# Causal scores masked after the exponential by GpSimd for two of four groups of heads, with small steps of the second attention layer moved

## What is computed

```python
q = q * cos + _rotate_half(q) * sin            # 16 heads of depth 8, 256 tokens
k = k * cos + _rotate_half(k) * sin
att = jnp.einsum('bhtd,bhsd->bhts', q, k) * scale
causal = jnp.tril(jnp.ones((T, T), dtype=bool))
att = jnp.where(causal, att, jnp.finfo(att.dtype).min)
att = jax.nn.softmax(att, axis=-1)
y = jnp.einsum('bhts,bhsd->bhtd', att, v)
y = y.transpose(0, 2, 1, 3).reshape(B, T, C)
return y @ w_proj
```

## Time and profile before

| | us |
|---|---|
| time before, median of 3 runs | 1256.86 (1255.71 to 1260.93) |
| the profiled execution's own time | 1255.29 |
| its span, first instruction to last | 1253.5 |
| PE busy | 1060.1 (85%) |
| DVE busy | 924.8 (74%) |
| ACT busy | 848.4 (68%) |
| POOL busy | 625.6 (50%) |

### The profile page before, as it was taken

How to read it: one execution, slowest core, us unless ns; L and a number is a source line. 1 busy time by engine, 2 the same in 40 slices (tenths; PEclk the granted TensorE clock), 3 DMA queues, 4 the chain that set the end, 5 groups by cost and what they waited for, 6 DMA issues and landing times. The chain is left out here.

```text
span 1253.5 us, 35551 instructions
## 1 busy us (share of the span) xinstructions
PE 1060.1 (85%) x11349; PEld 784.8 (63%) x11349; DVE 924.8 (74%) x2432; ACT 848.4 (68%) x1920; POOL 625.6 (50%) x894
## 2 busy tenths in 40 slices
PE   4699999999999999687899999999999996921420
PEld 3467666666667676365687877888778884511420
DVE  3488888888888888153577777777777773479895
ACT  2267777777777777473577887778877775632596
POOL 3245556655556553306355666556665531500494
PEclk9699999999999999798799999999999998865655
DMA  7555545555545552027656556555555540300013
GB/s 197 125 141 130 137 122 128 132 132 131 128 122 133 132 130 53 2 106 239 165 151 153 147 146 150 148 152 147 147 148 146 146 95 15 115 9 0 1 43 92
DMA packets 120217, 148.39 MB, mean 118 GB/s; under 512 B 12467, under 2 KB 99923, under 8 KB 110931
## 3 DMA queue, kind: packets, MB, share of 16 engines
q1 hardware_dynamic: 113362, 139.65, 44.0%
q10 hardware_dynamic: 6784, 7.86, 1.9%
HBM read 88.44 MB, written 45.35 MB: 107 GB/s over the span
## 5 line engine op out<-in xcount | busy, mean ns | idle before, releaser
L528 DVE TENSOR_REDUCE attn_negmax<-attn_row_ps 128x2 f32<-128x512 f32 (+1 forms) x1024 | 597.0, 618 | 189.0 <-PE attn_row_ps L718 177.8
L450 ACT ACTIVATE probs<-attn_col_ps 128x512 f32<-128x512 f32 (+1 forms) x1024 | 530.6, 541 | 129.9 <-PE attn_col_ps L740 122.1
L718 PE MATMUL attn_row_ps<-k_st,q_st 72*128 72x256 bf16 (+1 forms) x2048 | 369.5, 262 | 8.0 <-DMA k_st<-attn_scratch 8.0
L740 PE MATMUL attn_col_ps<-q_st,k_st 74*128 74x256 bf16 (+1 forms) x2048 | 367.4, 260 | 2.7 <-ACT probs L450 1.5
L757 PE MATMUL attn_out_ps<-probs,v_sb 128*32 128x256 f32 (+1 forms) x4096 | 228.5, 356 | 0.7 <-ACT probs L450 0.7
L740 PEld LDWEIGHTS attn_col_ps<-q_st,k_st 74*128 74x128 bf16 x2048 | 186.8, 98 | 63.7 <-ACT probs L450 30.3
L718 PEld LDWEIGHTS attn_row_ps<-k_st,q_st 72*128 72x128 bf16 x2048 | 201.1, 99 | 34.3 <-issue 8.6
L757 PEld LDWEIGHTS attn_out_ps<-probs,v_sb 128*32 128x32 f32 x4096 | 122.1, 109 | 67.5 <-issue 19.5
L736 PE MATMUL attn_col_ps<-mask_kq,ident_h 128*128 128x256 bf16 x512 | 141.6, 277 | 12.5 <-DMA q_st<-attn_mT_sb 6.7
L307 POOL TENSOR_SCALAR attn_var<-attn_mv 128x2 f32<-128x2 f32 x64 | 14.3, 223 | 274.6 <-DVE attn_mv L591 274.6
L714 PE MATMUL attn_row_ps<-mask_qk,ident_h 128*128 128x256 bf16 x512 | 141.8, 277 | 4.8 <-DMA k_st<-attn_scratch 4.7
(11 more groups left out here) (243 smaller groups left out, 1604.0 us busy)
## 6 DMA issues: line engine op xcount, KB each, us to landing
q_st<-attn_scratch SPq DMA_DIRECT2D x192, 192.0 KB
k_st<-attn_scratch SPq DMA_DIRECT2D x192, 192.0 KB
attn_scratch<-attn_parts SPq DMA_DIRECT2D x64, 384.0 KB, 2.8
attn_scratch<-attn_parts SPq DMA_DIRECT2D x64, 128.0 KB, 2.8
qk<-qk_scratch SPq DMA_DIRECT2D x29, 256.0 KB, 2.7
qk_scratch<-probs ACTq DMA_DIRECT2D x7, 1024.0 KB, 4.7
attn_xT<-x_mid SPq DMA_DIRECT2D x32, 128.0 KB, 2.4
attn_xT<-x_all SPq DMA_DIRECT2D x32, 128.0 KB, 2.4
```

The costliest lines, as they stand in the source:

```text
L450: nc.scalar.activation(probs_of(st, 3, u)[:, j, 0:W], col_ps[:, n % 2, 0:W], ACT.Exp, scale=scale).then_inc(probs_kept, 1)
L528: nc.vector.tensor_reduce(negmax[:, t, 2 * p:2 * p + 2], row_ps[:, row_bank(st, u), 0:2 * keys].rearrange("p (a k) -> p a k", a=2), AX_X, ...
L718: last = nc.tensor.matmul(bank[:, a * keys:(a + 1) * keys], q_st[0:KROWS, sl, h, t * P:(t + 1) * P], k_st[0:KROWS, sl, h, 0:keys], start=n ...
L740: last = nc.tensor.matmul(bank[:, t * N:(t + 1) * N - first], k_st[0:rows, sl, h, t * P:(t + 1) * P], q_st[0:rows, sl, h, first:N], start= ...
```

## The change

It does three things, all in the second layer's attention (line numbers of the new file are some 10 to 20 higher).

1. For units 0 and 1 (`sel={0: (1, 3), 1: (1, 3)}`) the column scores lose the mask product. In its place POOL sets the probabilities above the diagonal to zero after the exponential (`keep_seen`, one `affine_select` of 128 x 1024 float32 for each unit, in place). POOL does both in every step, for lag 3, right after L385, and waits for the unit's four exponentials before each. `sum_values` of these units waits for the select instead of the exponentials. Rows keep their mask, and so do the columns of units 2 and 3.
2. In `AT["attn1"]` small items move: ACT's `mT1` from place 0 to 2, `oT` from 2 and 4 to 3 and 4, `onT` from 13 to 10, `mT0` from 9 to 10, `half` from 3 and 5 to 6 and 7, `ln` from 8 to 13; PE's `v` from 3 to 7, `onT` from 13 to 10, `mT0` from 9 to 10, the sums of units 0 and 1 from 8 to 11 and of units 2 and 3 from 2 to 3.
3. `give={"ln": [1]}`: POOL no longer waits before "rest" and "lo". The operation "ln" is reached only where `ln_on` is "pool", and here it is "act", so nothing waits in its place.

```diff
-      "attn1": dict(act_mT1=0, act_oT=(2, 4), act_onT=13, act_mT0=9, act_v=8, act_half=(3, 5), act_ln=8, dve_o=6,
+      "attn1": dict(act_mT1=2, act_oT=(3, 4), act_onT=10, act_mT0=10, act_v=8, act_half=(6, 7), act_ln=13, dve_o=6,
                     dve_split0=8, dve_split1=15, dve_v=None, dve_y=15, dve_var=15, dve_ln=None, pe_mT1=2, pe_oT=6,
-                    pe_v=3, pe_onT=13, pe_mT0=9, pe_y=15, pe_pv={8: [(3, 0), (3, 1)], 2: [(4, 2), (4, 3)]},
-                    give={"lo": [0], "rest": [0]}, ln_lag=5, ln_on="act")}
+                    pe_v=7, pe_onT=10, pe_mT0=10, pe_y=15, pe_pv={11: [(3, 0), (3, 1)], 3: [(4, 2), (4, 3)]},
+                    give={"ln": [1]}, ln_lag=5, ln_on="act", sel={0: (1, 3), 1: (1, 3)})}
...
+            def keep_seen(st, place):
+                for u, (at_place, lag) in sorted(at["sel"].items(), key=lambda item: -item[1][1]):
+                    if at_place == place and st.has(lag):
+                        pool.wait_ge(probs_kept, st.seq(lag, H, 4 * u + 4))
+                        apart(pool, mem)
+                        diagonal = probs_of(st, lag, u).rearrange("p j (t q) -> p j t q", t=TB)[:, :, :, 0:P]
+                        nc.gpsimd.affine_select(out=diagonal, in_=diagonal, compare_op=ALU.is_ge, fill=0.0, base=0,
+                                                pattern=[[0, 4], [0, TB], [1, P]], channel_multiplier=-1)\
+                            .then_inc(seen_kept, 1)
...
                         pool.wait_ge(turned, st.seq(0, c=1))
+                keep_seen(st, 1)
+                if st.has(0):
                     if st.has(1):
...
-                if causal:
+                masked = causal and n // 4 not in at["sel"]
+                if masked:
...
-                                            start=not causal, stop=True, skip_group_check=causal)
+                                            start=not masked, stop=True, skip_group_check=masked)
...
-                pe.wait_ge(probs_kept, st.seq(lag, H, 4 * u + 4))
+                if u in at["sel"]:
+                    pe.wait_ge(seen_kept, st.seq(lag, SELECTED, sorted(at["sel"]).index(u) + 1))
+                else:
+                    pe.wait_ge(probs_kept, st.seq(lag, H, 4 * u + 4))
```

More of the change, by code:

```diff
@@ L37 @@
                     pe_pv={8: [(3, 0), (3, 1)], 14: [(3, 2)], 4: [(4, 3)]}, give={"ln": [1], "lo": [0]}, ln_lag=4,
-                    ln_on="pool"),
-      "attn1": dict(act_mT1=0, act_oT=(2, 4), act_onT=13, act_mT0=9, act_v=8, act_half=(3, 5), act_ln=8, dve_o=6,
+                    ln_on="pool", sel={}),
+      "attn1": dict(act_mT1=2, act_oT=(3, 4), act_onT=10, act_mT0=10, act_v=8, act_half=(6, 7), act_ln=13, dve_o=6,
                     dve_split0=8, dve_split1=15, dve_v=None, dve_y=15, dve_var=15, dve_ln=None, pe_mT1=2, pe_oT=6,
-                    pe_v=3, pe_onT=13, pe_mT0=9, pe_y=15, pe_pv={8: [(3, 0), (3, 1)], 2: [(4, 2), (4, 3)]},
-                    give={"lo": [0], "rest": [0]}, ln_lag=5, ln_on="act")}
+                    pe_v=7, pe_onT=10, pe_mT0=10, pe_y=15, pe_pv={11: [(3, 0), (3, 1)], 3: [(4, 2), (4, 3)]},
+                    give={"ln": [1]}, ln_lag=5, ln_on="act", sel={0: (1, 3), 1: (1, 3)})}
 HALF_ON = "act"
@@ L208, in head @@
             return NH * (u // 2) + 2 * j + u % 2
+        seen_kept, SELECTED = sem("seen_kept"), len(at["sel"])
         UNITS, ROW_BANKS = NH * TB, 3
@@ L361, in step @@
                         .then_inc(x_res_kept, 1)
+                keep_seen(st, 0)
                 if st.has(0):
@@ L396, in step @@
                     pool.wait_ge(rest_kept, st.seq(0, c=1))
+                keep_seen(st, 2)
+                if st.has(0):
                     apart(pool, mem)
@@ L403, in step @@
                         .then_inc(lo_kept, 1)
+                keep_seen(st, 3)
                 if LN == 4 and st.has(LN):
```

## The result

The changed kernel takes 1278.13 us (median of 4 runs, 1275.16 to 1282.08), the kernel before 1256.28 on the same chip (4 runs, 1251.38 to 1260.93): a ratio of 1.0178, with a 95% interval of 1.015 to 1.0206. It is slower by some 22 us, and the forecast was 1279. The profiled execution took 1280.3 us, its span is 1278.5 (before 1253.5).

A forecast was written before the change was run, and what follows sets the result against it. PE, busy 336.5 of 340 us, was taken as the bound. 29 steps x 0.8 = 23, less 1.5, on 1255.3 gave 1277; the median's 1.6 above made 1279 us, range 1241 to 1295.

The forecast's parts named there:

- The collision: DVE's split behind place 8 is held by both selects; PE's transposes of mT0 start at T+10.24 instead of 9.22.
- the walk: One changed step followed by instruction from T, PE's first column product: 15.0 to 15.1 us against 14.27, +0.8.
- A select like two inputs: Rival: a POOL select costs 2.52 us, PE waits 2.6 us more per step, some 1353 us; chance 0.06.
- The split slips through: Rival: the cast precedes the selects, one select holds the subtraction; step 14.2, 1252 us (1247 to 1260); chance 0.17.
- The masks: Eight PE mask products of 0.11 go per step, 0.89 us; 28 us over 32 sequences if nothing else were late.
- The wait before place 10: PE, done with places 8 and 9 at T+8.02, waits for exponential 8 until 8.50, behind both crosswise copies.
- The wait before place 6: After places 4 and 5, PE waits for exponential 4 until T+5.14.
- half of the removed time comes back as waiting: Plain run of places: two alternating banks need 1.00 us for two places without masks, PE's work 0.89.
- At place 3 the wait: PE's rows of place 3 need DVE's first reduction, so start at T+2.30; four masks bring nothing in the first quarter.
- the last three steps: Steps without rotary work on POOL or crosswise copies: nothing collides, some 0.5 each gained, -1.5 us.
- The DMAs: POOL's last part ends about 1.9 us later; stores, loads and stacking transfers slide, at no cost.
- The masks pay: Rival: shorter waits at places 3, 6 and 10, no collision; down to 1229 us, likelier 1242; chance 0.27.

The follow-up runs named there:

- number 4: The changed kernel with POOL waiting for DVE's first split before the two selects: 1260.33 us, 1.0033 of the kernel before.
- number 1: The changed kernel with DVE's first split one place earlier, behind place 7: 1258.77 us, 1.0028 of the kernel before.
- 8: The changed kernel with the split behind place 7, values at 2, crosswise copies and sums of units 0 and 1 at 12: 1278.34 us.
- number 5: The changed kernel with masks back on PE, no selects and POOL's old waits, so the moved places alone: 1265.10 us, 1.0083 of the kernel before.
- 7: number 4 with values projected at place 2, crosswise copies and sums of units 0 and 1 at 12: 1256.91 us.
- 10: number 4 with early places of the kernel before, crosswise copies and sums of units 0 and 1 at 12: 1254.47 us, 1.0000 of the kernel before.
- number 9: The kernel before without the column masks of units 0 and 1 and without selects, output not the reference's: 1248.82 us, 0.9944 of the kernel before.

## Why the prediction was right, point by point

**The collision: right in mechanism and place, a little too large.** Selects of 1.106 us (taken 1.20) stand back to back between L397 and L404; the cast was to start 0.26 inside the first and starts 0.08 to 0.49 inside; L558 ends 0.03 behind the second. The transposes of mT0 start at T+9.95 (walked 10.24, and 9.22 without a collision). In number 4 they start at T+9.63, 9.25 and 9.01 in the three steps of a turn, here at 10.19, 10.09 and 9.95: the collision costs 0.78 a step on average, where the walk has 1.02. With the collision taken away in two ways, 18 to 21 us go. The rule of the Trainium skill, page "SBUF — State Buffer", section "Who interferes with whom" (whoever comes second waits for the whole instruction), is borne out for a one-input select: number 1 shows L558 at 1.12 beside a select.

**A select like two inputs** is refuted by 1.106. So is, for this operation, the estimate of 1.54 from the Trainium skill, page "GPSIMD Engine Reference", section 3.1: the measurement decides. PE has its margin at the sums: those of unit 1 start 1.7 us behind the second select's end (the prediction says 0.7, and its own walk gives 10.96 + 0.70 - 10.06 = 1.6).

**"The split slips through" was decided by tenths**, as said, and in the step with the smallest margin by 0.08 us. That it was not let through is in part luck. Numbers 1 and 8 are the same split at place 7, once with two steps of three let through, once with none.

**The masks: right that they are mostly lost, with the waits at places 6 and 10 walked too long.** The wait before place 10 was walked at 0.48 and is 0.31 (1.43 from place 8 to place 10 where PE's own work, with masks, is 1.12). The record shows 0.16 of it: a gap between records is shorter than the delay between starts. The wait before place 6 was walked at 0.23 and is 0.10 to 0.13. A part of this is one reading that doesn't carry over: the prediction takes the 0.14 between an exponential's end and place 8 of the kernel before as the time in which a bank comes free. At places 6 and 10 of the changed kernel it is 0.05. So two places without masks are bound by 0.37 + 0.49 + 0.05 = 0.91 and not by 1.00, next to 0.89 of PE's own work, and "half of the removed time comes back as waiting" doesn't hold for a plain run of places. The waits read in the trace lie behind ACT's copies and behind DVE. At place 3 the wait was walked at 0.29 in every step. It is 0.06, 0.64 and 0.25 in the three steps of a turn of the loop, 0.32 on average. The long one (in the step from 829.26) has a cause that the walk didn't have, DVE's own pause:

```profile
830.80 0.25 DVE L608 BATCH_NORM_AGGREGATE attn_mv<-attn_stats 128x2 f32<-128x6 f32 x2
831.45 1.95 DVE L545 TENSOR_REDUCE attn_negmax<-attn_row_ps 128x2 f32<-128x256 f32 x4 [0.40 <-issue]
```

It stands idle for 0.40 for nothing that the profile shows, once in three steps, which fits the end of the loop's turn. The kernel before has the same pause; the releaser that the profile names there, and in number 5, had long been done:

```profile
816.73 1.35 DVE L528 TENSOR_REDUCE attn_negmax<-attn_row_ps 128x2 f32<-128x256 f32 x3 [0.40 <-PE attn_row_ps L718]
```

In the changed kernel, PE then:

```profile
831.93 0.28 PE L731 MATMUL attn_row_ps<-mask_qk,ident_h 128*128 128x256 bf16 x1 [0.48 <-DVE attn_negmax L545]
```

Before, PE did the sums at this moment and rows needed DVE only behind them. Moving the sums behind place 3 took that cover away. That the moves cost by themselves is shown (number 5, +9 us). In number 5 the rows of place 3 start 0.46, 0.12 and 0.01 late in the three steps, 0.20 a step in all, and the pause is at most 0.15 of the 0.29 by which a step is longer. Besides, the transposes of mT1 and the sums, which no longer follow each other, take PE 0.25 more together, place 10 comes 0.09 later, and 0.30 of waiting before place 8 is gone. These are read from the distances between PE's starts and not tested one by one.

**The sum's terms.** Per step +0.8 was walked; measured is 15.18 - 14.26 = +0.92, or 24.5 over the 29 steps where 23 were taken. The step without a collision was set too low: 14.2 said, and by the walk's own terms it is 15.08 - 1.02 = 14.06; measured are 14.37 to 14.40. So "slips through" would have given 1256 to 1260, not 1252. For the last three steps 0.5 each was expected; two distances went from 13.94 to 13.75, 0.2 each. The walk's +0.8 is 1.02 for the collision less 0.2 for the rest; measured are 0.78 and +0.14. Two errors, 0.24 and 0.35 a step or 7 and 10 us over 29 steps, have opposite signs, so 1279 for 1278.1 is in part luck.

**The DMAs: right.** No row of PE's waits in the changed kernel between 700 and 965 us names a transfer. POOL's last part ends 1.75 later in the step (walked 1.9). In numbers 7 and 10, where the crosswise copies stand at 12, some do; the cover was not large.

**The masks pay** was the largest rival at 0.27, down to 1229. Even with nothing in the masks' place (number 9) the time is 1248.8. The rival's own value of 1242 was still too hopeful.

**The accounts.** Moves alone with the old waits: +9 us (5). Masks traded for selects that wait: 5 us back, to +4 (4). No wait: 18 more, to +22.

## What to carry to other kernels

Work that is handed to GpSimd has two prices: its duration, and what small VectorE instructions on the critical chain lose when they start inside it. Two GpSimd instructions in a row can take the wait of each of two dependent VectorE instructions, 2 us for 0.37 of work here; a semaphore wait that lets them through first took the loss away (18 us better) and cost nothing as long as the next user of the result came late enough, whereas a favourable place in the order didn't survive the next edit. Before taking work from an engine that is 99% busy, look at what it would wait for next at each joint: of 28 us of removed matmuls, 7 came back as time.

## What the runs showed of the hardware

- An affine select on GpSimd of 128 x 1024 float32, in place, takes 1.106 us, two in a row 2.16. By the small selects of the earlier trace rows it was 1.20.
- A one-input GpSimd select holds VectorE's two-input instruction to its end and 0.02 to 0.03 us beyond (1.02 to 1.12 us for one of 0.17), and holds a cast of 0.16 for up to 1.06. The cast has one input only.
- Two PSUM banks between TensorE and ScalarE: from the first matmul of a head without a mask to its exponential 0.37, the exponential of 128 x 384 0.49, from its end to the matmul that waited for the bank 0.05 (822.40 to 822.45 in the changed kernel). An estimate from these is 0.91 us for two places, however little TensorE has to do. No two such places follow in less than 0.98 in any run: the exponential of place 0 starts 0.44 to 0.46 and not 0.37 behind its first matmul. A ScalarE copy in between comes on top: in number 9 place 8 waits, until 829.86, for an exponential that started at 829.22, behind the second crosswise copy. Of the 28 us of masks taken from a TensorE that had been busy for 99% of the stretch, 7 came back.
- VectorE's stream pauses for 0.40 us once per turn of the loop in every kernel here, the one before included (from 816.33 to 816.73). The profile names "issue" in most of them. Whether it matters depends on what TensorE needs from it just then.
